# Second-half low parts on VectorE from PSUM, GpSimd on adjacency tiles alone, with counts, routing and fills moved (graph layer and expert layer, one core)

## The chip, the cores and the metric

One core of one Trainium2 chip runs the kernel. The metric is the device time of one launch in microseconds; the profiled execution has a span (first to last instruction) and a time with what lies around the span.

## The reference, cut to what matters

2048 rows of 256 values pass through a graph layer and then through an expert layer: each row goes to one of 8 experts (top 1 of the logits), and to a shared feed-forward layer of width 1024 besides.

```python
def layer(x, adj, W, b, gate_w, w1, w2, w3, sw1, sw2):
    deg = maximum((adj != 0).sum(-1), 1)
    xn = layernorm(x)
    pooled = rsqrt(deg) * ((adj + I) @ xn) * rsqrt(deg) + xn
    x = x + relu(pooled @ W + b)
    xf = layernorm(x)                                   # 2048 x 256
    w, idx = top_1(xf @ gate_w.T)                       # of 8 experts, weight softmax(w)
    y = sum_e [idx == e] * ((silu(xf @ w1[e].T) * (xf @ w3[e].T)) @ w2[e].T)
    y = y + gelu(xf @ sw1.T) @ sw2.T                    # the shared layer, width 1024
    return x + y
```

## The kernel before

**High and low parts.** Matmuls take fp32r operands, so an operand is split: ScalarE copies it to an fp32r tile (the high part), VectorE or GpSimd subtracts that from the original (the low part), and TensorE multiplies both. All that GpSimd splits has its original in SBUF.

**Tiles.** 2048 rows are NT = 16 tiles of 128, in NQ = 4 quarters. Quarter q of the graph layer sums over the 16 adjacency tiles (128x512 each): `adj_highs` on ScalarE (L667), `adj_lows` on GpSimd (L477), `agg_part` on TensorE (L1304 and L1306). Tiles 0 to 7 of quarters 2 and 3 are split ahead, in the shared stage before (LEAD = 8; AR = 4 of them in the first ring of slots). The raw tiles come two to a DMA ("chunk", NC = 8 a quarter) into RAW = 4 slots on SP's queue; a slot comes free when the low parts of its tiles are done and VectorE has counted it (`count_chunks`, L922 for the first chunk of a quarter and L925 for the others), so a late count delays a load.

**Order on TensorE.** Quarter 0, then for q = 1, 2, 3: quarter q of the sums (`agg_quarter`, with the transposes of the layer-normed rows of quarter q - 1 ahead of tile 12, L1262), gate, degrees, and for q = 1 and 2 a *shared stage* of 16 blocks of the shared layer (blocks 0 to 15, 16 to 31); after quarter 3 the last stage of 32 blocks (32 to 63, LAST = 32), with the routing of the last rows. Then 23 expert steps.

**A block m of the shared layer** is 128 columns of the width for 256 rows: `shared_up` (6 matmuls, L1405) into PSUM, gelu into `gel` (ScalarE, L726), its high part `gel_hi` (ScalarE, L730), its low part `gel_lo` (GpSimd, L490, from `gel` in SBUF), `shared_down` (4 matmuls, L1427 and L1429). TensorE issues up(m), down(m - 2), up(m + 1), and so on; `gel_hi` of block m waits until down(m - 2) is done, and the buffers hold two blocks. In a shared stage ScalarE and GpSimd do two blocks and then one adjacency tile of the next quarter, eight times.

**VectorE in a shared stage** finishes the graph layer, reads logits (`choose`), ranks (`read_ranks`) and positions (`place_rows`), adds the shared result of the first half to the rows (`add_shared`, L1042 and L1049), counts the first three chunks of the next quarter and adds the second half. In the quarter that follows it makes the variances of the rows (L860, L865), waits for the roots (`stds`, ScalarE L641), scales, adds the bias (L916) and counts on. ScalarE does `stds` after its tile 11 and then four `scaled_rows` (L647).

**GpSimd at the end of quarters 2 and 3** scatters four tiles of rows to `sorted_x` (L554) ahead of the next shared stage's first low part.

**The last stage.** GpSimd makes the low parts of blocks 32 to 55, with scatters between, and VectorE those from LAST + DVE_AT on. VectorE also splits chunks 0 to 7 of expert 0 (`low_chunk`, L1155), GpSimd the rest (`low`, L520). The routing tables end with `routed`. SP loads expert chunks (L417; each waits until an earlier chunk has been split, `elo_ok`), writes 8 fill blocks into `sorted_x` (L409) ahead of chunk MORE = 8, and loads the sorted rows of steps 0 to 2 (L425) behind chunks 11, 12 and 13, after waiting for `routed`, the scatters (L421) and the fills. TensorE transposes the rows of step 0 (L1262) ahead of block 63's up.

## Time and profile before

| | us |
|---|---|
| median of 3 runs (475.58 to 478.83) | 475.96 |
| time of the profiled execution | 476.37 |
| its span | 474.6 |
| TensorE matmul busy | 445.6 (94%) |
| GpSimd busy | 322.6 (68%) |
| VectorE busy | 255.2 (54%) |
| ScalarE busy | 208.4 (44%) |
| first shared stage | 81.3 to 109.3 |
| second shared stage | 134.4 to 163.2 |
| last shared stage | 188.4 to 241.0 |

The times of the stages are from the span's start. TensorE is the busiest engine nearly everywhere, so what counts is where it stands idle and who ends its wait. Matmuls overlap, so a stage's length is read from the starts of its matmuls and not from their busy time.

### The profile page before, as it was taken

The numbers are of one execution on the slowest core, as the hardware profiler recorded it, in microseconds if no ns is written. First come the engines' busy times: TensorE is split into PE (matmuls) and PEld (weight loads), VectorE is DVE, ScalarE is ACT, GpSimd is POOL, SyncE is SP. The second block draws the span as 40 slices with busy tenths as digits, with TensorE's granted clock in tenths as the row PEclk, the third lists the DMA queues.
The fourth block names the chain that finished last, engine by engine and source line by source line (L and its number), as shares of the span: only waits on it lengthen the run. The fifth ranks groups of instructions, "written<-read, shape, count | busy, mean of one in ns | idle before, by whom it ended". The sixth has DMA issues, their size and how long they took to land.

```text
span 474.6 us, 8852 instructions
## 1 busy us (share of the span) xinstructions
PE 445.6 (94%) x2635; PEld 381.7 (80%) x2636; DVE 255.2 (54%) x540; ACT 208.4 (44%) x462; POOL 322.6 (68%) x296
## 2 busy tenths in 40 slices
PE   7889999989999899999898999999999999999992
PEld 6779777878888788888787888888888888888872
DVE  5884979663767455888934433343334334433430
ACT  4777596655456354645442323232323222322330
POOL 3548975897488765779875498885677579883112
PEclk9999999999999899999999999999999999999997
DMA  8555534130440407685665999997898552663000
GB/s 272 205 176 182 159 107 136 55 110 24 134 135 1 134 2 254 228 310 207 195 200 151 377 353 378 339 341 240 305 330 303 184 203 36 75 79 44 2 0 0
DMA packets 39612, 82.61 MB, mean 174 GB/s; under 512 B 5024, under 2 KB 14752, under 8 KB 37536
## 3 DMA queue, kind: packets, MB, share of 16 engines
q1 hardware_dynamic: 27024, 47.60, 30.8%
q0 software_dynamic: 7536, 29.39, 20.2%
q10 hardware_dynamic: 5024, 5.27, 3.6%
q8 instruction: 15, 0.25, 0.2%
q14 instruction: 13, 0.11, 0.1%
HBM read 74.74 MB, written 8.41 MB: 175 GB/s over the span
## 4 chain that ended last, share of the span: by engine, by line
PE 72%; POOL 11%; DVE 6%; ACT 4%; issue 3%; DMA 2%; SPq 1%; POOLq 0%; ACTq 0%; DVEq 0%
PE bank L1486 26%; PE bank L1513 9%; PE bank L1304 9%; PE bank L1514 5%; PE bank L1306 4%; PE bank L1499 4%; POOL gel_lo L490 4%; PE bank L1405 4%; PE bank L1427 3%; PE bank L1262 2%; POOL a_lo L477 2%; POOL ering L520 2%; PE bank L1429 1%; PE bank L1288 1%; POOL sorted_x L554 1%
## 5 line engine op out<-in xcount | busy, mean ns | idle before, releaser
L1486 PE MATMUL bank<-ering,xsT_hi 128*128 x368 | 121.7, 402 | 1.4 <-POOL ering L520 1.4
L477 POOL TENSOR_TENSOR a_lo<-araw,a_hi 128x512 fp32r<-128x512 f32 x48 | 69.9, 1467 | 28.4 <-ACT a_hi L667 27.8
L1220 DVE SCALAR_TENSOR_TENSOR hid<-bank,xs,sil 128x512 f32<-128x512 f32 x46 | 34.5, 751 | 93.9 <-ACT sil L803 93.9
L1486 PEld LDWEIGHTS bank<-ering,xsT_hi 128*128 128x128 f32 x368 | 69.4, 189 | 17.8 <-issue 1.9
L1486 PE MATMUL bank<-ering,xsT_lo 128*128 x184 | 73.0, 396 | 0.0
L1304 PE MATMUL bank<-zz,a_hi 128*128 128x512 f32 x192 | 69.9, 404 | 2.4 <-POOL a_lo L477 2.4
L803 ACT ACTIVATE sil<-bank 128x512 f32<-128x512 f32 x46 | 27.5, 598 | 101.4 <-PE bank L1486 101.4
L520 POOL TENSOR_TENSOR ering<-eraw,ering 128x512 fp32r<-128x512 f32 x40 | 51.4, 1303 | 29.2 <-DMA ering<-in_experts 20.3
L1513 PE MATMUL bank<-ering,hidT_hi 128*128 x184 | 67.5, 407 | 1.2 <-DVE hidT_lo L1228 1.2
L520 POOL TENSOR_TENSOR ering<-eraw_more,ering 128x512 fp32r<-128x512 f32 x48 | 60.6, 1292 | 8.3 <-PE bank L1262 5.1
L625 POOL DMA_INDIRECT out<-y_rows,row_token x23 | 35.8, 1554 | 36.8 <-DVE y_rows L1236 31.4
L1427 PE MATMUL bank<-sw_r,gel_hi 128*128 128x512 f32 x128 | 50.4, 415 | 8.7 <-POOL gel_lo L490 6.9
L1306 PE MATMUL bank<-zz,a_lo 128*128 128x256 f32 x192 | 53.8, 280 | 0.0
L490 POOL TENSOR_TENSOR gel_lo<-gel,gel_hi 128x256 fp32r<-128x256 f32 x56 | 43.2, 778 | 14.9 <-ACT gel_hi L730 14.3
L1514 PE MATMUL bank<-ering,hidT_lo 128*128 x184 | 51.7, 281 | 0.0
L1304 PEld LDWEIGHTS bank<-zz,a_hi 128*128 128x128 f32 x192 | 36.1, 188 | 11.6 <-POOL a_lo L477 2.8
L1513 PEld LDWEIGHTS bank<-ering,hidT_hi 128*128 128x128 f32 x184 | 34.6, 188 | 8.7 <-issue 1.4
L925 DVE SCALAR_TENSOR_TENSOR count<-araw,count 128x1024 bf16<-128x1024 f32 x28 | 40.0, 1428 | 1.6
L1486 PEld LDWEIGHTS bank<-ering,xsT_lo 128*128 128x128 f32 x184 | 34.8, 189 | 7.3
L1405 PE MATMUL bank<-xfT_hi,sw_hi 128*128 128x256 f32 x128 | 37.3, 292 | 0.0
L1427 PEld LDWEIGHTS bank<-sw_r,gel_hi 128*128 128x128 f32 x128 | 24.7, 193 | 15.1 <-POOL gel_lo L490 6.7
L730 ACT ACTIVATE gel_hi<-gel 128x256 fp32r<-128x256 f32 x64 | 26.8, 418 | 22.5 <-PE bank L1429 22.2
(165 smaller groups left out, 931.1 us busy)
## 6 DMA issues: line engine op xcount, KB each, us to landing
araw<-in_adj_t SPq DMA_DIRECT2D x32, 512.0 KB, 4.5
eraw<-in_experts SPq DMA_DIRECT2D x48, 256.0 KB, 4.7
ering<-in_experts POOLq DMA_DIRECT2D x8, 1536.0 KB, 9.3
eraw_more<-in_experts SPq DMA_DIRECT2D x48, 256.0 KB, 5.9
ering<-in_experts POOLq DMA_DIRECT2D x8, 1024.0 KB, 7.1
ering<-in_experts POOLq DMA_DIRECT2D x8, 512.0 KB, 5.2
xs<-sorted_x ACTq DMA_DIRECT2D x20, 129.0 KB, 3.7
sw_raw<-in_sw_t ACTq DMA_DIRECT2D x2, 1024.0 KB, 7.5
```

Source lines behind the costliest of these rows:

```text
L477: pool.tensor_tensor(lo_part(s), araw[:, u // CJ, u % CJ, :], hi_part(s).bitcast(F32), ALU.subtract).then_inc(adj_lo_ok, 1)
L490: pool.tensor_tensor(gel_lo[:, u, :], gel[:, u, :], gel_hi[:, u, :].bitcast(F32), ALU.subtract).then_inc(sh_lo, 1)
L520: pool.tensor_tensor(ering[:, slot, 1, c * ECW:(c + 1) * ECW], raw, ering[:, slot, 0, c * ECW:(c + 1) * ECW].bitcast(F32), ALU.subtract).t ...
L625: pool.indirect_dma_start(out=out, out_offset=bass.IndirectOffsetOnAxis(ap=row_token[:, s:s + 1], axis=0), in_=y_rows[:, s, :], in_offset= ...
L925: dve.scalar_tensor_tensor(into, araw[:, r, :, :], 0.0, into, ALU.not_equal, ALU.add).then_inc(adj_counted, CJ)
L1304: pe.matmul(acc(q, it)[:, :], hi_part(s)[:, it * P:(it + 1) * P], zt, start=first, stop=False)
L1306: ins = pe.matmul(acc(q, it)[:, 0:D], lo_part(s)[:, it * P:(it + 1) * P], zt[:, 0:D], start=False, stop=False)
L1405: ins = pe.matmul(up_bank(m)[:, 0:HALF], w[:, k, ib * P:(ib + 1) * P], a[:, q % 2, k, half * HALF:(half + 1) * HALF], start=n == 0, stop=n ...
L1427: pe.matmul(shared_bank(hq, k)[:, :], gel_hi[:, m % 2, k * P:(k + 1) * P], sw2_r[:, ib, :, :].rearrange("p h d -> p (h d)"), start=ib == 0 ...
L1486: ins = pe.matmul(bank[2 * w + h][:, :], a[:, k, :], ering[:, bass.ds(slot, 1), part, at:at + BANK].rearrange("p a n -> p (a n)"), start=n ...
L1513: pe.matmul(bank[6][:, :], hidT_hi[:, k, :], w2, start=k == 0, stop=False)
L1514: ins = pe.matmul(bank[6][:, 0:D], hidT_lo[:, k, :], ering[:, bass.ds(slot, 1), 0, W2AT + k * D:W2AT + (k + 1) * D].rearrange("p a n -> p ...
```

## The change

- Blocks 8 to 15 of each of the first two shared stages: gelu goes to PSUM (`gel_in`, two banks that are free then), ScalarE makes `gel_hi` from there, and VectorE the low part (`shared_lows_from_psum`). GpSimd makes the low parts of blocks 0 to 7 alone, and after them `exp_of_z` and adjacency tiles 3 to 7.
- VectorE's order in these stages: the first half's sums are spread between the low parts, and the three counts come after the last low part.
- In quarters 2 and 3 ScalarE does `stds` ahead of tile 8 and the scaled rows after tiles 9 and 10; VectorE adds the bias after the count of chunk 3 and not before it.
- Last stage: GpSimd also makes the low parts of blocks 56 and 57 (DVE_AT 24 to 26). VectorE adds the shared result of the sixth half-quarter and splits chunks 4 to 7 before the later part of the routing tables.
- SP: three fills stay ahead of chunk 8, five go ahead of chunk 20; the sorted rows of steps 0 to 2 are loaded behind chunks 13, 14 and 15. ScalarE waits for all fills before its loop over the steps.

```diff
--- before.py
+++ after.py
@@ -183,9 +183,10 @@
     LAST = (NQ - 2) * 2 * NI
 
     EARLY_RANKS_AT, THIRD_RANKS_AT, XF_AT, GATE_AT, RANKS_AT = 9, 9, 8, 11, 14
-    DVE_AT = 24
+    DVE_AT = 26
     EARLY, MORE = 4, 8
-    FIRST_AT, FIRST_ROWS = EC - 1, 3
+    FIRST_AT, FIRST_ROWS = EC + 1, 3
+    FILLS_AT = 2 * EC - ER
     STORE_FROM = 3 * EC + ER
 
     with ExitStack() as ctx:
@@ -220,6 +221,10 @@
 
             stage = min(m // (2 * NI), NQ - 2)
             return bank[(4 if m >= (2 * NQ - 1) * NI else other(stage + 1)) + m % 2]
+
+        def gel_in(m):
+
+            return acc(m // (2 * NI) + 1, 1 - m % 2)[:, 0:HALF]
 
         def shared_bank(hq, k):
 
@@ -402,9 +407,9 @@
                 for c in range(EC):
                     n = e * EC + c
 
-                    if n == MORE:
+                    if n == MORE or n == FILLS_AT:
                         sp.wait_ge(counted, 1)
-                        for a in range(E):
+                        for a in range(FIRST_ROWS) if n == MORE else range(FIRST_ROWS, E):
                             row = sp.value_load(fill_row[0:1, a:a + 1], min_val=0, max_val=SPARE - P)
                             sp.dma_start(sorted_x[bass.ds(row, P), :], pad_row[:]).then_inc(filled, 16)
                     slot, to = raw_at(e, c)
@@ -418,7 +423,7 @@
                     if n == FIRST_AT:
                         sp.wait_ge(routed, 1)
                         sp.wait_ge(scattered, 16 * NT)
-                        sp.wait_ge(filled, 16 * (E + 1))
+                        sp.wait_ge(filled, 16 * (1 + FIRST_ROWS))
                     if FIRST_AT <= n < FIRST_AT + FIRST_ROWS:
                         i = n - FIRST_AT
                         row = sp.value_load(step_row[0:1, i:i + 1], min_val=0, max_val=SPARE)
@@ -562,12 +567,15 @@
                 if q >= 2:
                     scatter(q - 2, 0, QT)
                 if q < NQ - 1:
-                    for j in range(LEAD):
+                    pool.wait_ge(sh_lo, (q - 1) * 2 * NI)
+                    for j in range(AR):
                         shared_lows((q - 1) * 2 * NI + 2 * j, 2)
-                        adj_lows(q + 1, j, j + 1)
-                        if j == AR - 1:
-                            exp_of_z(q - 1)
-
+                        if j < AR - 1:
+                            adj_lows(q + 1, j, j + 1)
+                    exp_of_z(q - 1)
+                    adj_lows(q + 1, AR - 1, LEAD)
+
+            pool.wait_ge(sh_lo, LAST)
             shared_lows(LAST, 2)
             pool.wait_ge(agg_sum, NQ)
             pool.wait_ge(adj_counted, NQ * NT)
@@ -606,6 +614,7 @@
             scatter(3, 2, 3)
             shared_lows(LAST + 22, 2)
             scatter(3, 3, 4)
+            shared_lows(LAST + 24, 2)
 
             pool.wait_ge(elo_ok, MORE)
             for c in range(MORE, EC):
@@ -718,6 +727,21 @@
                                    xf_bank(q, b)[:, :].rearrange("p (t k n) -> p t k n", t=2, k=KD),
                                    ACT.Copy).then_inc(xfT_hi_ok, 1)
 
+            def shared_blocks_in_psum(first, n):
+
+                for m in range(first, first + n):
+                    q = m // (2 * NI) + 1
+                    if m % NI == 0:
+                        act.wait_ge(agg_free, (q + 1) * QT)
+                    if m % NI == 1:
+                        act.wait_ge(rank_read, q)
+                    act.wait_ge(sh_ps, m + 1)
+                    act.wait_ge(sh_lo, m - 1)
+                    act.activation(gel_in(m), up_bank(m)[:, 0:HALF], ACT.Gelu).then_inc(sh_gelu, 1)
+                    act.wait_ge(sh_gelu, m + 1)
+                    act.wait_ge(sh_used, m - 1)
+                    act.activation(gel_hi[:, m % 2, :], gel_in(m), ACT.Copy).then_inc(sh_hi, 1)
+
             def shared_blocks(first, n):
                 def one(u, m, early):
                     act.wait_ge(sh_ps, m + 1)
@@ -760,15 +784,17 @@
             for q in range(1, NQ):
                 if q == 1:
                     split_gate()
+                if q > 1:
+                    stds(NQ + q - 1)
                 for j in range(ring(q), NT - 1 if q == 1 else NT):
                     adj_highs(q, j, j + 1)
                     if q == 1 and AR + 2 <= j < AR + 10:
                         shared_piece_high(j - AR - 2)
-                    if j == ring(q) + 3:
+                    if q == 1 and j == AR + 3:
                         stds(NQ + q - 1)
-                    if ring(q) + 4 <= j < ring(q) + 6:
+                    if AR + 4 <= j < AR + 6 and q == 1 or LEAD + 1 <= j < LEAD + 3 and q > 1:
                         for i in range(2):
-                            scaled_rows((q - 1) * QT + 2 * (j - ring(q) - 4) + i, NQ + q - 1)
+                            scaled_rows((q - 1) * QT + 2 * (j - (AR + 4 if q == 1 else LEAD + 1)) + i, NQ + q - 1)
                 xfT_highs(q - 1)
                 if q == 1:
                     adj_highs(q, NT - 1, NT)
@@ -779,7 +805,10 @@
                     act.dma_start(sorted_x[SPARE:SPARE + P, :], pad_row[:]).then_inc(filled, 16)
                 if q < NQ - 1:
                     for j in range(LEAD):
-                        shared_blocks((q - 1) * 2 * NI + 2 * j, 2)
+                        if j < AR:
+                            shared_blocks((q - 1) * 2 * NI + 2 * j, 2)
+                        else:
+                            shared_blocks_in_psum((q - 1) * 2 * NI + 2 * j, 2)
                         adj_highs(q + 1, j, j + 1)
             shared_blocks(LAST, XF_AT)
             xfT_highs(NQ - 1)
@@ -832,6 +861,7 @@
             silus(0)
             rows_high(2)
             hid_highs(0)
+            act.wait_ge(filled, 16 * (1 + E))
             with act.Fori(0, (STEPS - 3) // XR) as i:
                 for u in range(XR):
                     step(i * XR + (1 + u), (1 + u) % XR)
@@ -1035,6 +1065,12 @@
                 settle()
                 dve.tensor_tensor(at, part(0), at, ALU.add).then_inc(logit_ok, 1)
 
+            def shared_lows_from_psum(first, n):
+                for m in range(first, first + n):
+                    dve.wait_ge(sh_hi, m + 1)
+                    dve.tensor_tensor(gel_lo[:, m % 2, :], gel_in(m), gel_hi[:, m % 2, :].bitcast(F32),
+                                      ALU.subtract).then_inc(sh_lo, 1)
+
             def first_sums(hq):
 
                 dve.wait_ge(sh_used, (hq + 1) * NI)
@@ -1108,11 +1144,11 @@
                 scales(NQ + q - 1)
                 if q == 1:
                     shared_pieces(1, 3)
-                else:
-                    add_bias(q)
                 count_chunks(q, 3, RAW)
                 if q == 1:
                     shared_pieces(3, 5)
+                else:
+                    add_bias(q)
                 count_chunks(q, RAW, RAW + 1)
                 if q == 1:
                     shared_pieces(5, 7)
@@ -1138,9 +1174,17 @@
                 logits(q - 1)
                 if q < NQ - 1:
                     choose(q - 1)
+                    second_half = (2 * q - 1) * NI
+                    dve.wait_ge(sh_lo, second_half)
+                    shared_lows_from_psum(second_half, 1)
                     read_ranks(q - 1)
+                    shared_lows_from_psum(second_half + 1, 1)
                     place_rows(q - 1)
-                    add_shared(2 * (q - 1))
+                    shared_lows_from_psum(second_half + 2, 1)
+                    first_sums(2 * (q - 1))
+                    shared_lows_from_psum(second_half + 3, 1)
+                    second_sums(2 * (q - 1))
+                    shared_lows_from_psum(second_half + 4, NI - 4)
                     count_chunks(q + 1, 0, 3)
                     add_shared(2 * (q - 1) + 1)
             choose(NQ - 2)
@@ -1178,6 +1222,9 @@
             step(dve.tensor_tensor(r_e[:, :, 0:E], per_e(tiles[:], E), upto[:], ALU.mult))
             step(dve.tensor_reduce(ends[:], r_e[:, :, 0:E], AX_X, ALU.add))
 
+            add_shared(2 * NQ - 3)
+            for c in range(EARLY, MORE):
+                low_chunk(c)
             step(dve.tensor_tensor(r_s[:], per_e(ends[:], STEPS), s_iota[:], ALU.is_le))
             step(dve.tensor_reduce(step_f[:], r_s[:], AX_X, ALU.add))
             step(dve.tensor_scalar(step_i[:], step_f[:], float(E - 1), None, ALU.min))
@@ -1198,9 +1245,6 @@
                                   xsT_hi[:].bitcast(F32), ALU.subtract).then_inc(xsT_lo_ok, 1)
                 dve.tensor_copy(row_token[:, bass.ds(n - 1, 1)], xs[:, u, D:D + 1]).then_inc(token_ok, 1)
 
-            for c in range(EARLY, MORE):
-                low_chunk(c)
-            add_shared(2 * NQ - 3)
             dve.wait_ge(sh_lo, LAST + DVE_AT)
             for m in range(LAST + DVE_AT, NB):
                 if m == NB - 2:
@@ -1208,9 +1252,9 @@
                 dve.wait_ge(sh_hi, m + 1)
                 dve.tensor_tensor(gel_lo[:, m % 2, :], gel[:, m % 2, :], gel_hi[:, m % 2, :].bitcast(F32),
                                   ALU.subtract).then_inc(sh_lo, 1)
+                if m == LAST + DVE_AT:
+                    first_sums(2 * NQ - 2)
                 if m == LAST + DVE_AT + 1:
-                    first_sums(2 * NQ - 2)
-                if m == LAST + DVE_AT + 2:
                     second_sums(2 * NQ - 2)
 
 
```

## Rows read from the trace of the kernel before

**Rows 1.** Busy time of each engine by stretch: two shared stages, quarter 2 between them.
```profile
81.30:109.27 27.97, 24.94 (x186) 22.10 (x182) 16.98 (x38) 16.71 (x41) 24.00 (x25) 1.00 0.31 97
109.27:134.43 25.16, 25.16 (x154) 21.49 (x153) 14.60 (x26) 11.72 (x22) 14.70 (x12) 1.00 0.29 85
134.43:163.24 28.81, 26.11 (x185) 23.18 (x182) 16.96 (x38) 16.76 (x41) 25.23 (x27) 0.94 0.28 91
```

**Rows 2.** Timeline of TensorE, first stage: start, duration, instruction, [idle before <- releaser].
```profile
95.04 0.39 PE L1427 MATMUL bank<-sw_r,gel_hi 128*128 128x512 f32 x1
...
95.73 0.28 PE L1405 MATMUL bank<-xfT_hi,sw_hi 128*128 128x256 f32 x1
...
104.69 0.50 PE L1427 MATMUL bank<-sw_r,gel_hi 128*128 128x512 f32 x1 [1.77 <-POOL gel_lo L490]
...
110.66 0.40 PE L1304 MATMUL bank<-zz,a_hi 128*128 128x512 f32 x1
```

**Rows 3.** Timeline of GpSimd, second half of the first stage.
```profile
100.69 2.28 POOL L477 TENSOR_TENSOR a_lo_more<-araw,a_hi_more 128x512 fp32r<-128x512 f32 x1
102.94 2.39 POOL L490 TENSOR_TENSOR gel_lo<-gel,gel_hi 128x256 fp32r<-128x256 f32 x2
```

**Rows 4.** Timeline of VectorE, second half of the first stage.
```profile
99.00 1.11 DVE L922 TENSOR_SCALAR count<-araw 128x1024 bf16<-128x1024 f32 x1
100.25 3.81 DVE L925 SCALAR_TENSOR_TENSOR count<-araw,count 128x1024 bf16<-128x1024 f32 x2
```

**Rows 5.** Groups by form: x count | busy us, mean ns | idle before.
```profile
L1197 DVE TENSOR_TENSOR xsT_lo<-bank,xsT_hi 128x256 fp32r<-128x256 f32 x23 | 9.6, 415 | 1.9 <-ACT xsT_hi L797 1.9
...
L1209 DVE TENSOR_TENSOR gel_lo<-gel,gel_hi 128x256 fp32r<-128x256 f32 x8 | 6.2, 784 | 1.7 <-ACT gel_hi L730 1.7
...
L730 ACT ACTIVATE gel_hi<-gel 128x256 fp32r<-128x256 f32 x64 | 26.8, 418 | 22.5 <-PE bank L1429 22.2
...
L667 ACT ACTIVATE a_hi<-araw 128x512 fp32r<-128x512 f32 x48 | 29.9, 628 | 14.5 <-PE bank L1306 14.5
```

**Rows 6.** Timeline of VectorE, start of quarter 2.
```profile
109.47 0.76 DVE L1042 TENSOR_TENSOR resid<-bank,resid 128x256 f32<-128x256 f32 x2 [5.42 <-PE bank L1429]
...
112.36 0.38 DVE L865 BATCH_NORM_AGGREGATE mv<-stats 128x2 f32<-128x6 f32 x4
```

**Rows 7.** Timeline of ScalarE, quarter 2.
```profile
115.73 1.28 ACT L641 ACT_TABLE_LOAD   x1
117.03 0.30 ACT L641 ACTIVATE std<-mv,eps 128x4 f32<-128x4 f32 x1
```

**Rows 8.** Chain that ended last, in order of time: transposes ahead of tile 12.
```profile
126.08 0.87 PE bank L1262 x8
```

**Rows 9.** Timeline of GpSimd, quarter 2 and the start of the second stage.
```profile
119.46 1.55 POOL L477 TENSOR_TENSOR a_lo_more<-araw,a_hi_more 128x512 fp32r<-128x512 f32 x1 [0.23 <-ACT a_hi_more L667]
127.32 2.54 POOL L477 TENSOR_TENSOR a_lo_more<-araw,a_hi_more 128x512 fp32r<-128x512 f32 x2 [6.31 <-ACT a_hi_more L667]
...
136.34 1.45 POOL L490 TENSOR_TENSOR gel_lo<-gel,gel_hi 128x256 fp32r<-128x256 f32 x2 [0.51 <-ACT gel_hi L730]
```

**Rows 10.** Timeline of TensorE, last stage: block 56's down, step 0's rows.
```profile
232.87 0.47 PE L1427 MATMUL bank<-sw_r,gel_hi 128*128 128x512 f32 x1 [1.57 <-DVE gel_lo L1209]
...
239.30 0.38 PE L1262 MATMUL bank<-ident,xs 128*128 128x128 f32 x2
```

**Rows 11.** Timeline of VectorE, last stage: chunks 4 to 7.
```profile
225.87 4.14 DVE L1155 TENSOR_TENSOR ering<-eraw,ering 128x512 fp32r<-128x512 f32 x4
```

**Rows 12.** Timeline of GpSimd, last stage: chunks 8 to 11.
```profile
231.19 5.56 POOL L520 TENSOR_TENSOR ering<-eraw,ering 128x512 fp32r<-128x512 f32 x4 [0.92 <-DMA eraw<-in_experts]
```

**Rows 13.** Timeline of SP's queue, last stage: eight fills, sorted rows of step 0.
```profile
218.29 8.85 SPq L409 DMA_DIRECT2D sorted_x<-pad_row  x8
...
234.12 0.34 SPq L425 DMA_DIRECT2D xs<-sorted_x  x1
```

**Rows 14.** DMA issues between 228 and 240: x count, KB, median us to landing.
```profile
xs<-sorted_x SPq DMA_DIRECT2D x3, 129.0 KB, 3.8
```

## Prediction

> **What bounds the kernel now.** I read first the busy shares by stretch: a shared stage takes 27.97 us the first time and 28.81 the second, and TensorE is idle for part of both; in the quarter between them, 25.16, it is not [rows 1]. Then TensorE's own timeline: from block 7's down at 95.04 to block 10's up at 95.73 a down takes 0.69, an up the same, so a block is worth 1.40; but block 12's down waits 1.77 for a low part of GpSimd [rows 2]. GpSimd's and VectorE's timelines beside it say why: GpSimd's adjacency tile takes 2.28, where two take 2.54 in the quarter [rows 9], and its next two low parts 2.39, while VectorE's two counts stretch to 3.81, where the first count, which has one input in SBUF, takes 1.11 [rows 3, 4]. The reader is to see in these rows a stage that GpSimd bounds, and two engines that hold each other up just where GpSimd has no time to spare. The second stage's granted clock is 0.94 [rows 1]: for a while TensorE ran at 1.2 and not 2.4 GHz, after the same wait.
>
> **Stage one.** From 95.04 on TensorE has downs 7 to 15 and ups 10 to 15 to do: 15 pieces of 0.70 are 10.5. The last down must wait for its own high and low part behind block 13's down, with one down of cover: high part 0.42, low part 0.415 [rows 5], some 0.3 of signals (my estimate from the gaps between such instructions) make 1.15; less 0.70, 0.45 is exposed. 95.04 + 10.5 + 0.45 + 0.1 = 106.1, where the quarter now starts at 109.27 [rows 1]: **-3.15**. The low part's price decides: VectorE takes 415 ns for 128x256 with one operand in PSUM, 784 ns from two SBUF tiles [rows 5]. I take the first, whose form this is; the upper bound too fits into 1.40 and would cost 0.4 once a stage. What VectorE does between the low parts (positions some 2 us, sums 0.76 a pair [rows 6]) fits: I find block 10's low part, behind `place_rows`, within 0.1 of its due time, all others early. ScalarE has two passes of 0.42 a block and a tile of 0.63 every second block [rows 5], 2.3 in 2.8.
>
> On the low part's form the Trainium skill speaks against the change: "VectorE: DVE Perf Modes", the section on the TRN2 errata, gives VectorE 62 cycles more per operation from PSUM than from SBUF, an estimate of 0.065 us a block. By that rule the stage would lose 0.065 more at its last block; by the rows nothing.
>
> **Stage two.** The same, and the low clock goes with the wait that I take for its cause: 28.81 - (27.97 - 3.15) = **-4.0**. If the wait isn't its cause it stays: 0.85 less gain [rows 1].
>
> **Quarters 2 and 3, where the counts go.** T is a quarter's start. VectorE ends its last low part at T - 0.9, the first count (1.11) at T + 0.25; one GpSimd tile (the seventh, from T - 0.8) is in the way until T + 0.5, then come two counts of 1.25 each (3.81 less a tile of 1.27, halved [rows 4, 9]), to T + 3.0. Sums and variances took 3.27 from 109.47 to 112.74 [rows 6], so they end at T + 6.3, 2.8 later than now. ScalarE's roots now stand ahead of tile 8, behind them ScalarE's high parts, behind those GpSimd's low parts and TensorE. The table load of 1.28 stands ahead of the root and needs nothing from VectorE (115.73, then the root at 117.03 [rows 7]), so it is long done: tile 8's high part starts at T + 6.6, its low part could at T + 7.2. Beside GpSimd's tiles VectorE then counts chunk 3, adds the bias and counts twice. A count costs GpSimd 1.0 (2.28 less 1.27 [rows 3, 9]), an add at most 0.28 (1.55 less 1.27 [rows 9]). Tile 14's low part ends at 7.2 + 1.0 + 7 x 1.25 + 4 x 0.28 + 2 x 1.0 = T + 20.1. TensorE wants it at 14 x 1.39 + 0.87 = T + 20.3 (110.66 less 109.27 for a tile [rows 1, 2]; transposes [rows 8]). It holds by 0.2. Tile 15 ends at T + 21.3; now it ends at 129.86, T + 20.6, and the scatters behind it were done 0.51 before the second stage's first low part [rows 9], so they come 0.2 to 0.3 late: +0.3 a quarter. Bounds: nothing, if the adds slip between; if each count blocks for its whole 1.25 and each add for 0.3, tile 14 ends at T + 20.8, 0.5 late, and the scatters take 0.35 more: +0.85 a quarter. So 0.6 to 1.7 for both, and I take **+1.1**, the middle, as 2.39 less 1.45 for two low parts (0.94 [rows 3, 9]) points to the lower end and 3.81 to the upper.
>
> The Trainium skill's "SBUF — State Buffer", Who interferes with whom, has the two engines exclude each other when VectorE reads two SBUF inputs and GpSimd reads SBUF, the second fully blocked. By it the quarters would cost 1.7. The trace's 3.81 for two counts agrees, its 1.0 per count on GpSimd is a little less.
>
> What costs nothing: chunk 7 is loaded when chunk 3 has been counted, at T + 8.2 and now near T + 13.3, so GpSimd's tiles 14 and 15 no longer wait for it (6.31 idle now [rows 9]). Were that later again, it would be on TensorE at once.
>
> **The last stage.** GpSimd's last scatter ends at 231.19 - 0.92 = 230.3 [rows 12], block 56's low part follows at once, and TensorE's wait of 1.57 [rows 10] goes: its down comes at 231.15 and not 232.87, and step 0's transposes could come at 237.6 and not 239.30. But they need the sorted rows of step 0, and these move behind two more chunks on SP; chunk 12 waits for chunk 8's split, chunk 13 for chunk 9's. GpSimd now first does blocks 56 and 57 (to 231.9, all in old times), then four chunks at 1.39 [rows 12]: chunk 9's split ends at 234.8, SP issues chunk 13, reads the row number and issues the load at 236.0, now 234.12 [rows 13]. With 3.8 to landing [rows 14] that is 239.8: TensorE waits 2.2, and step 0 begins 0.5 later than now, though all before it was 1.7 early. Bounds by a landing 1 us faster or slower: -0.5 to +1.5. Splitting chunks 4 to 7 (4.14 beside GpSimd [rows 11]) moves to where GpSimd has blocks and scatters without a gap: I add 0.3 (bounds 0 and 1). For TensorE's 2.2 us of idleness I add 0.4, half the price of the low clock above, since it came after one of two long waits. Together **+1.2**. Hidden: the routing tables end 5.7 later, near 225.9 + 5.7 = 231.6 [rows 11], still ahead of the load; the five fills (8.85 for eight [rows 13], 1.1 each) stand ahead of chunk 20, the down weights of expert 1, due behind step 2's up. Without that cover the fills would cost 5.5. The steps themselves are untouched.
>
> **Sum.** -3.15 - 4.0 + 1.1 + 1.2 = -4.85 against the profiled execution's 476.37, which lies 0.4 above the median. I take the difference over: 475.96 - 4.85 = 471.1.
>
> **Rivals.**
> 1. *The quarters give the gain back* (0.22). For it: 0.2 of slack at tile 14. If the first count too excludes GpSimd's seventh tile, everything moves by 1.2 more on top of the upper bound: 2.0 a quarter, 4.0 and not 1.1, 474.0. Against it: the first count stayed at 1.11 beside GpSimd's work [rows 4].
> 2. *The sorted rows land in time* (0.18): then the last stage gives -0.4 and no low clock, 1.6 less than my +1.2: 469.5. For it: the landing alone decides, and 1 us of it does half.
> 3. *VectorE's low parts are late* (0.08): `place_rows` reads two SBUF inputs twice and may wait 1.27 for a tile [rows 9]; block 10 is 1.3 late in each stage: 473.7.
> 4. *Slower* (0.07): ScalarE's root becomes the wait. From variances at T + 6.6 on each microsecond later goes onto TensorE, in both quarters. At T + 9.0 they have eaten the 4.85; at T + 11.5 it is 480.9. Against it: VectorE's 3.27 [rows 6] meets nothing of GpSimd's.
> 5. *The change doesn't do what it says* (0.03): ScalarE's passes through PSUM are so slow that ScalarE bounds the stages as GpSimd did: 476.5. Against it: it has 0.5 to spare in 2.8.
>
> **How the numbers follow.** My own case has 0.42 and runs from 469.8 to 472.6. The range runs from below rival 2, 468.0, over rivals 1 and 3 to 474.8; rivals 4 and 5 and the ends of the others are left out, under 0.2. Within 1% (4.76 us, about what a measurement of this kernel can tell from no change) begins at 471.2. Below it lie 0.26 of my own case's 0.42 and all of rival 2: 0.44. Slower by over 1% is the far part of rival 4 and what I don't see: 0.04. The rest, 0.52, is within 1%.
>
> **What the profile would show.** Right: first stage near 24.8, second the same at clock 1.00; VectorE's low parts at 0.42; quarters of 25.2 to 26; TensorE waiting about 2 us for a DMA at step 0's transposes; ScalarE idle some 6 us ahead of its root. Wrong: quarters above 26.5 with TensorE waiting for tiles 9 to 14 (rival 1), no wait at step 0 (rival 2), block 10's down a microsecond late (rival 3), a second stage still at clock 0.94.

## The result and the profile after

| | before | after |
|---|---|---|
| median, us | 477.22 (11 runs, 475.51 to 481.15) | 472.80 (11 runs, 471.62 to 475.31) |
| ratio to before | | 0.9902, 95% interval 0.988 to 0.9924 |
| profiled execution: time, span | 476.37, 474.6 | 472.11, 470.4 |

The changed kernel is faster by 0.98%, 4.4 us by the medians and 4.26 by the profiled executions; forecast were 4.85. That lies just inside the 1% to which the forecast gave 0.52. The forecast time was 471.1 and the measured one is 472.80: 0.4 of the difference is the smaller gain and 1.3 the kernel before, whose median is 477.22 over 11 runs and was 475.96 over the three that the forecast started from.

The busy times by stretch, cut at the starts of TensorE's stages (columns as in [rows 1]: stretch, length, then busy time and count of TensorE's matmuls, its weight loads, VectorE, ScalarE, GpSimd, granted clock, DMA share, GB/s):

```profile
81.58:106.50 24.92, 24.18 (x184) 21.95 (x181) 15.64 (x45) 16.93 (x42) 16.34 (x17) 1.00 0.15 48
106.50:132.26 25.76, 25.53 (x154) 21.48 (x153) 22.32 (x28) 10.59 (x22) 18.47 (x11) 1.00 0.47 152
132.26:157.50 25.24, 24.15 (x184) 21.93 (x181) 15.65 (x45) 17.09 (x42) 18.25 (x19) 1.00 0.09 34
157.50:183.23 25.73, 25.49 (x155) 21.61 (x153) 22.34 (x28) 10.57 (x22) 18.39 (x12) 1.00 0.52 170
183.23:234.45 51.22, 47.89 (x356) 42.69 (x352) 44.37 (x106) 25.29 (x63) 44.23 (x51) 1.00 0.65 220
```

The stages that took 27.95 and 28.81 take 24.92 and 25.24, and the clock of the second is 1.00. The quarters between them, 25.16 and 25.15 before, have grown to 25.76 and 25.73. What TensorE still waits for at the places that the change touched and ahead of step 1, from its timeline (start, duration, instruction, idle before and who ended it):

```profile
105.69 0.50 PE L1471 MATMUL bank<-sw_r,gel_hi 128*128 128x512 f32 x1 [0.29 <-DVE gel_lo L1071]
128.65 0.51 PE L1348 MATMUL bank<-zz,a_hi_more 128*128 128x512 f32 x1 [0.23 <-POOL a_lo_more L482]
135.46 0.47 PE L1471 MATMUL bank<-sw_r,gel_hi 128*128 128x512 f32 x1 [0.80 <-POOL gel_lo L495]
...
186.30 0.47 PE L1471 MATMUL bank<-sw_r,gel_hi 128*128 128x512 f32 x1 [0.58 <-POOL gel_lo L495]
...
234.45 0.44 PE L1306 MATMUL bank<-ident,xs 128*128 128x128 f32 x2 [1.66 <-DMA xs<-sorted_x]
...
247.00 0.50 PE L1530 MATMUL bank<-ering,xsT_hi 128*128 x1 [1.37 <-issue]
```

The wait of 1.77 in the stage is gone; 0.29 is left at its last down. Three new ones stand in its place: tile 15 of each quarter (128.65, and the same at 179.66), the first low part of the next stage (0.80 and 0.58; it was 0.39 and 0.37), and the sorted rows of step 0 (1.66). The last line, the pause ahead of the loop over the steps, is not new: it was 1.38 before. The first two new ones have one source, which GpSimd's and VectorE's timelines of quarter 2 show side by side:

```profile
113.94 6.44 POOL L482 TENSOR_TENSOR a_lo<-araw,a_hi 128x512 fp32r<-128x512 f32 x4 [6.56 <-ACT a_hi L676]
120.34 8.25 POOL L482 TENSOR_TENSOR a_lo_more<-araw,a_hi_more 128x512 fp32r<-128x512 f32 x4
128.79 1.97 POOL L559 DMA_INDIRECT sorted_x<-rows,pos  x1 [0.19 <-issue]
...
133.60 0.96 POOL L559 DMA_INDIRECT sorted_x<-rows,pos  x1 [0.30 <-issue]
```

```profile
106.37 3.46 DVE L955 SCALAR_TENSOR_TENSOR count<-araw,count 128x1024 bf16<-128x1024 f32 x2
...
112.63 0.38 DVE L895 BATCH_NORM_AGGREGATE mv<-stats 128x2 f32<-128x6 f32 x4
...
113.69 1.23 DVE L955 SCALAR_TENSOR_TENSOR count<-araw,count 128x1024 bf16<-128x1024 f32 x1
114.83 5.83 DVE L946 TENSOR_TENSOR rows<-rows,bias 128x256 f32<-128x256 f32 x4
120.59 4.53 DVE L955 SCALAR_TENSOR_TENSOR count<-araw,count 128x1024 bf16<-128x1024 f32 x2
...
126.24 3.43 DVE L955 SCALAR_TENSOR_TENSOR count<-araw,count 128x1024 bf16<-128x1024 f32 x2
```

GpSimd begins tile 8 only at T + 7.44 (T = 106.50), 6.56 idle, and from there VectorE is in its way nearly all the time: four tiles take 6.44 and the next four 8.25, where a tile alone is 1.27 [rows 9]. Four bias adds take 5.83, 1.46 each, where one took 0.42 alone (at 117.65 in the kernel before): each ends about 0.3 after the tile beside it, so it was held until that tile was done. The last tile ends at T + 22.1, and the fourth scatter leaves at 134.56, when the stage has long begun.

### The profile page after: what moved, and what is told of

It reads as the page before. It is cut to its first block, busy times and chain, and to the rows that moved or that the text cites. A ratio compares the mean times of both kernels' runs of the same rounds, so it can differ in the third digit from the quotient of the medians.

```text
span 470.4 us, 8858 instructions
## 1 busy us (share of the span) xinstructions
PE 444.2 (94%) x2635; PEld 380.3 (81%) x2636; DVE 269.1 (57%) x554; ACT 206.8 (44%) x462; POOL 318.2 (68%) x282
## 3 DMA queue, kind: packets, MB, share of 16 engines
q0 software_dynamic: 7536, 29.39, 20.3%
## 4 chain that ended last, share of the span: by engine, by line
PE 66%; POOL 13%; DVE 10%; ACT 4%; issue 3%; DMA 2%; POOLq 0%; SPq 0%; DVEq 0%; ACTq 0%
PE bank L1530 28%; PE bank L1557 9%; PE bank L1449 5%; PE bank L1558 5%; PE bank L1543 4%; POOL a_lo L482 4%; PE bank L1471 4%; POOL a_lo_more L482 3%; PE bank L1348 3%; POOL sorted_x L559 2%; POOL gel_lo L495 2%; PE bank L1473 2%; PE bank L1306 2%; DVE stats L890 2%; DVE count L955 2%
## 5 line engine op out<-in xcount | busy, mean ns | idle before, releaser
L482 POOL TENSOR_TENSOR a_lo<-araw,a_hi 128x512 fp32r<-128x512 f32 x48 | 72.4, 1524 | 37.2 <-ACT a_hi L676 37.1
L1471 PE MATMUL bank<-sw_r,gel_hi 128*128 128x512 f32 x128 | 48.6, 402 | 3.5 <-POOL gel_lo L495 2.8
L955 DVE SCALAR_TENSOR_TENSOR count<-araw,count 128x1024 bf16<-128x1024 f32 x28 | 44.4, 1585 | 1.3
L495 POOL TENSOR_TENSOR gel_lo<-gel,gel_hi 128x256 fp32r<-128x256 f32 x42 | 31.2, 750 | 12.4 <-ACT gel_hi L754 11.6
L1350 PEld LDWEIGHTS bank<-zz,a_lo 128*128 128x128 f32 x192 | 36.3, 189 | 0.0
L1473 PE MATMUL bank<-sw_r,gel_lo 128*128 128x256 f32 x128 | 35.9, 281 | 0.0
```

The source lines that it names most:

```text
L482: pool.tensor_tensor(lo_part(s), araw[:, u // CJ, u % CJ, :], hi_part(s).bitcast(F32), ALU.subtract).then_inc(adj_lo_ok, 1)
L495: pool.tensor_tensor(gel_lo[:, u, :], gel[:, u, :], gel_hi[:, u, :].bitcast(F32), ALU.subtract).then_inc(sh_lo, 1)
L955: dve.scalar_tensor_tensor(into, araw[:, r, :, :], 0.0, into, ALU.not_equal, ALU.add).then_inc(adj_counted, CJ)
L1350: ins = pe.matmul(acc(q, it)[:, 0:D], lo_part(s)[:, it * P:(it + 1) * P], zt[:, 0:D], start=False, stop=False)
L1471: pe.matmul(shared_bank(hq, k)[:, :], gel_hi[:, m % 2, k * P:(k + 1) * P], sw2_r[:, ib, :, :].rearrange("p h d -> p (h d)"), start=ib == 0 ...
L1473: ins = pe.matmul(shared_bank(hq, k)[:, 0:D], gel_lo[:, m % 2, k * P:(k + 1) * P], sw2_r[:, ib, 0, :], start=False, stop=ib == NI - 1)
```

## The experiments

All kernels measured, by stretch. "Last" is from the last stage's start to step 0's up, "0 to 2" and "2 to 6" from the up of one step to that of the other, all in the profiled execution; then its time and the median of all runs of that kernel.

| kernel | stage 1 | quarter 2 | stage 2 | quarter 3 | last | 0 to 2 | 2 to 6 | profiled | median |
|---|---|---|---|---|---|---|---|---|---|
| before | 27.95 | 25.16 | 28.81 | 25.15 | 52.64 | 20.19 | 38.23 | 476.37 | 477.22 |
| after | 24.92 | 25.76 | 25.24 | 25.73 | 53.13 | 20.17 | 38.42 | 472.11 | 472.80 |
| e1 | 24.87 | 25.76 | 25.27 | 25.76 | 51.70 | 20.24 | 39.36 | 471.36 | 472.10 |
| e2 | 24.90 | 25.47 | 25.01 | 25.57 | 54.77 | 21.71 | 38.13 | 473.66 | 472.07 |
| e3 | 24.87 | 25.59 | 24.88 | 25.48 | 52.94 | 21.71 | 38.13 | 472.49 | 472.40 |
| e4 | 26.04 | 26.08 | 26.43 | 26.06 | 54.13 | 22.19 | 38.38 | 477.57 | 477.02 |
| e5 | 24.92 | 25.75 | 25.34 | 25.76 | 53.33 | 21.67 | 38.10 | 473.43 | 473.34 |
| e6 | 24.91 | 25.77 | 25.24 | 25.74 | 52.86 | 21.65 | 38.14 | 472.31 | 471.73 |
| e7 | 24.91 | 25.74 | 25.26 | 25.77 | 51.63 | 21.82 | 38.17 | 472.72 | 472.24 |
| e8 | 24.91 | 25.47 | 24.87 | 25.47 | 51.63 | 21.77 | 39.19 | 473.62 | 471.11 |
| e9 (after again) | 24.91 | 25.76 | 25.24 | 25.71 | 53.46 | 21.70 | 38.11 | 474.89 | 474.89 |
| e10 | 24.91 | 25.27 | 25.19 | 25.16 | 51.54 | 20.34 | 39.24 | 470.59 | 470.97 |
| e11 | 24.91 | 25.27 | 24.91 | 25.27 | 51.61 | 20.24 | 38.34 | 469.27 | 469.63 |

The last two columns alone would mislead. The table shows which stretch an edit touched; "0 to 2" is 20.2 or 21.7 for a reason of its own (e9), and in e2 and e4 the same reason lengthens "last".

**e1: sorted rows one chunk earlier.**

```diff
-    FIRST_AT, FIRST_ROWS = EC + 1, 3
+    FIRST_AT, FIRST_ROWS = EC, 3
```

> The changed kernel with one edit: the sorted rows of steps 0 to 2 are loaded one chunk of the expert weights earlier on SP's queue. Theory: the 1.66 us that TensorE waits for a DMA at step 0's transposes come from the place of this load alone; the routing tables end at 228.35 and the load can go out near 229.2 and not 231.03, lands near 232.7, and the transposes begin near 232.8 and not 234.45. All of the 1.6 stays to the end: profiled time about 470.5 for 472.1. Rival: what is late next (the expert weights split by GpSimd, or the steps' own rows) takes it back: the transposes come earlier, step 0's up or step 1's does not, gain under 0.5.

The load left at 229.29 and not 231.03, the wait of 1.66 was gone, and "last" fell by 1.43. But the time fell by 0.75 only: steps 2 to 6 took 0.94 more. TensorE's timeline, the steps that lost (windows, columns as above), and GpSimd's timeline ahead of step 6:

```profile
264.51:274.43 9.92, 9.79 (x53) 8.03 (x52) 3.95 (x8) 3.28 (x8) 8.10 (x7) 1.00 1.05 384
283.99:294.33 10.34, 9.76 (x52) 8.05 (x51) 4.37 (x9) 3.68 (x8) 8.88 (x9) 1.00 1.00 352
```

```profile
294.33 0.50 PE L1530 MATMUL bank<-ering,xsT_hi 128*128 x1 [0.58 <-POOL ering L525]
```

```profile
285.90 1.29 POOL L525 TENSOR_TENSOR ering<-eraw,ering 128x512 fp32r<-128x512 f32 x1 [1.44 <-DMA ering<-in_experts]
...
288.97 6.26 POOL L525 TENSOR_TENSOR ering<-eraw_more,ering 128x512 fp32r<-128x512 f32 x5
```

Step 6 waits for the eighth chunk of an expert to be split, GpSimd waits for that expert's weights to land, and the DMA engines have a share of 1.0 meanwhile. The theory held up to step 0. Something late did take gain back, as the rival had it, but not where it looked: steps 0 and 1 began earlier, and the loss is ahead of steps 4 and 6, with a gain of 0.75 left and not under 0.5.

**e2: the root behind tile 11.**

```diff
-                if q > 1:
-                    stds(NQ + q - 1)
...
-                    if q == 1 and j == AR + 3:
+                    if j == ring(q) + 3:
                         stds(NQ + q - 1)
-                    if AR + 4 <= j < AR + 6 and q == 1 or LEAD + 1 <= j < LEAD + 3 and q > 1:
+                    if ring(q) + 4 <= j < ring(q) + 6:
...
```

> The changed kernel, but ScalarE's root in quarters 2 and 3 stands behind its high part of tile 11 again, and the scaled rows behind tiles 12 and 13. VectorE's order is that of the changed kernel. Theory: what makes the quarters 0.6 long is GpSimd's late start, since tile 8's high part waits behind a root that waits for the variances (T + 6.5), while its data are there near T + 4; with the root behind, GpSimd starts tile 8 near T + 4.2 and not T + 7.4, has 3 us of slack against the counts, the quarters go back to 25.2 and the scatters end before the next stage's first low part: 1.2 to 1.8 less than the changed kernel, about 470.6. Rival: the root is needed where it is, because count 3 and the load of chunk 7 hang on it: quarters 25.8 or longer, no gain or a loss.

GpSimd's timeline and TensorE's only wait from quarter 2 to the second stage's first downs:

```profile
110.56 2.55 POOL L482 TENSOR_TENSOR a_lo<-araw,a_hi 128x512 fp32r<-128x512 f32 x2 [3.60 <-ACT a_hi L676]
114.05 2.54 POOL L482 TENSOR_TENSOR a_lo<-araw,a_hi 128x512 fp32r<-128x512 f32 x2 [0.94 <-ACT a_hi L676]
116.70 3.63 POOL L482 TENSOR_TENSOR a_lo_more<-araw,a_hi_more 128x512 fp32r<-128x512 f32 x2
122.34 3.52 POOL L482 TENSOR_TENSOR a_lo_more<-araw,a_hi_more 128x512 fp32r<-128x512 f32 x2 [2.01 <-ACT a_hi_more L676]
```

```profile
134.51 0.47 PE L1469 MATMUL bank<-sw_r,gel_hi 128*128 128x512 f32 x1 [0.44 <-POOL gel_lo L495]
```

Tile 8 starts at T + 4.5 (T = 106.07), the first four tiles cost 1.27 each, no tile is late and the scatters leave in time. Yet the quarter took 25.47, not 25.16: TensorE's first twelve tiles took 16.97 where the changed kernel's took 16.65, without a wait in either. That is a rate, not a stall (see the end); less that 0.32, the quarter is 25.15. The whole from stage 1 to the last stage was 0.70 shorter; twice 0.3 of rate on top, the order is worth 1.3, the lower part of what was expected. e11 had the same order without that rate: 25.27, 24.91, 25.27, 1.29 less than the changed kernel.

The profiled time is nevertheless 1.55 longer than the changed kernel's, and not 470.6 as expected. Step 1's low clock (e9) adds 1.54 to it, and "last" took 1.64 more: the wait for the sorted rows was 2.00 there, and behind it TensorE's clock fell, which it did not behind the 1.66 of the changed kernel:

```profile
233.84 0.69 PE L1304 MATMUL bank<-ident,xs 128*128 128x128 f32 x2 [2.00 <-DMA xs<-sorted_x]
```

```profile
234.00:237.00 3.00, 3.00 (x13) 2.81 (x14) 0.91 (x3) 1.46 (x4) 2.83 (x3) 0.50 0.88 280
```

From these transposes to step 0's up it is 3.05, and 1.91 in the changed kernel. Of the six kernels with this wait (1.54 to 2.00), e2 and e4 (1.93) show the low clock behind it, e9 (1.94), e5 (1.85), the changed kernel and e3 do not.

**e3: counts with one input.** Chunks 3 to 7 of quarters 2 and 3 are counted without adding to what was counted, so degrees and rows differ from the reference's.

```diff
-                if first:
+                if first or (q >= 2 and n >= q * NC + 3):
+                    dve.wait_ge(adj_counted, n * CJ)
                     dve.tensor_scalar(into, araw[:, r, :, :], 0.0, None, ALU.not_equal)
```

> The changed kernel, but in quarters 2 and 3 the counts of chunks 3 to 7 are done in the form of the first count, which has one input in SBUF and does not add to what was counted: the degrees, and with them the rows, are not the reference's. Everything else, waits too, stays. Theory (VectorE's two inputs in SBUF and GpSimd exclude each other): a GpSimd tile beside such a count takes 1.3 again, the four tiles of 6.44 and the four of 8.25 become about 6 and 5.3, a count takes 0.7 to 1.1; quarters 25.2, scatters on time, 1.2 to 1.8 less than the changed kernel. Rival (any access of VectorE to SBUF holds GpSimd up, or the late root alone makes the stall): tiles as before, quarters still 25.7.

GpSimd's timeline, then VectorE's:

```profile
114.22 5.92 POOL L482 TENSOR_TENSOR a_lo<-araw,a_hi 128x512 fp32r<-128x512 f32 x4 [6.55 <-ACT a_hi L676]
120.10 6.10 POOL L482 TENSOR_TENSOR a_lo_more<-araw,a_hi_more 128x512 fp32r<-128x512 f32 x4
```

```profile
120.34 3.47 DVE L953 TENSOR_SCALAR count<-araw 128x1024 bf16<-128x1024 f32 x2
...
126.21 1.51 DVE L953 TENSOR_SCALAR count<-araw 128x1024 bf16<-128x1024 f32 x2
```

The stretch of two counts in the first line has a gap of 0.14 in it: they took 1.78 and 1.56. With the late root kept, cheaper counts alone brought GpSimd's last tile forward from T + 22.1 to T + 19.4; no tile and no scatter was late (25.59 less 0.32 of the same rate is 25.27). So lateness is start plus contention, and either half undone is enough. But the theory's reason was wrong by half: one-input counts do wait for tiles, 1.78 and 1.56 beside them and 0.68 alone, and the tiles they met took 1.73 where one alone is 1.27. They cost GpSimd less because they are shorter (0.7 and not 1.2), not because they leave it alone. The Trainium skill says as much in "SBUF — State Buffer", Who interferes with whom: a one-input `tensor_scalar` in a mode that uses both ports takes the shared pair too, and whoever comes second is blocked for the whole instruction; the rows agree.

**e4: GpSimd keeps all low parts, counts still behind them.** GpSimd's and ScalarE's orders in the stages are those of the kernel before; the lines shown are VectorE's.

```diff
-                    dve.wait_ge(sh_lo, second_half)
-                    shared_lows_from_psum(second_half, 1)
...
-                    shared_lows_from_psum(second_half + 4, NI - 4)
+                    dve.wait_ge(sh_lo, second_half + NI)
                     count_chunks(q + 1, 0, 3)
```

> The changed kernel, but all low parts of the first two shared stages stay with GpSimd, from SBUF, two blocks and a tile in turn, as in the kernel before; VectorE's three counts still come after the last low part, and quarters and last stage are those of the changed kernel. Theory: the stages gained from two things, and the counts' move is the larger: without them beside it GpSimd needs 1.45 for two low parts and 1.27 for a tile, 2.72 in 2.8 us of TensorE, so a stage takes 25.3 to 26 (27.95 and 28.81 before, 24.92 and 25.24 in the changed kernel). Rival: GpSimd cannot keep up even alone (its 2.72 leave nothing for the signals between it and ScalarE), and the low parts' move is what was needed: stages of 27 or more.

Stages of 26.04 and 26.43, at clock 1.00: of the 3.03 and 3.57 that the stages gained, 1.9 and 2.4 come from taking three counts out of GpSimd's way (0.86 of the 2.4 is the low clock of the kernel before), 1.1 and 1.2 from VectorE's low parts. That is the worth of the second move with the first one made; the low parts moved alone, with the counts left in the stage, were not run. Neither pure theory: GpSimd alone nearly keeps up, and where exp_of_z (1.05) or the end of the stage meets it, TensorE waits 0.4 to 0.5. Its quarters, 26.08 and 26.06, are the longest of all; the first count there begins at T - 0.76, beside a tile, and takes 1.71, so that all behind it comes later. Over the whole kernel little is left: its median, 477.02 over 10 runs, is 0.7 below that of the kernel before in the same session (ratio 0.9971, interval 0.9943 to 0.9998). With the quarters and the last stage as changed, the counts' move alone earns little more than they cost.

**e5: VectorE's low parts from SBUF.**

```diff
-                    dve.tensor_tensor(gel_lo[:, m % 2, :], gel_in(m), gel_hi[:, m % 2, :].bitcast(F32),
+                    dve.tensor_tensor(gel_lo[:, m % 2, :], gel[:, m % 2, :], gel_hi[:, m % 2, :].bitcast(F32),
...
```

> The changed kernel, but in blocks 8 to 15 of the first two stages gelu goes to SBUF as before, and VectorE makes the low parts from two SBUF tiles. Theory: it is the form with one operand in PSUM that keeps a low part at 0.42; from SBUF every second one meets a GpSimd tile and takes 0.8 to 1.3 (784 ns on average in the last stage [rows 5]), which reaches the path of TensorE's downs: stages of 25.2 to 26 in place of 24.9 and 25.2, GpSimd's tiles above 1.3. Rival: the cover of one down (0.7) hides that, and PSUM isn't needed: stages within 0.1 of the changed kernel's.

VectorE's timeline, two blocks of the first stage:

```profile
100.97 0.73 DVE L1068 TENSOR_TENSOR gel_lo<-gel,gel_hi 128x256 fp32r<-128x256 f32 x1 [0.17 <-ACT gel_hi L754]
102.37 0.42 DVE L1068 TENSOR_TENSOR gel_lo<-gel,gel_hi 128x256 fp32r<-128x256 f32 x1 [0.67 <-ACT gel_hi L754]
```

The mechanism is there, 0.73 beside a tile and 0.42 without, and it costs nothing that shows: 24.92 and 25.34, and GpSimd's tiles stay at 1.29 to 1.30. The last low part of a stage, the only one without cover, met no tile. The rival is right, and PSUM is not what made the gain.

**e6: the last stage as before.**

```diff
-    DVE_AT = 26
+    DVE_AT = 24
-    FIRST_AT, FIRST_ROWS = EC + 1, 3
+    FIRST_AT, FIRST_ROWS = EC - 1, 3
...
-            shared_lows(LAST + 24, 2)
```

> The changed kernel with the last stage of the kernel before (GpSimd's low parts to block 55, all eight fills ahead of chunk 8, sorted rows behind chunks 11 to 13, VectorE's order). Theory: the 1.57 of wait at block 56 is back, the wait for the sorted rows at step 0 is gone; last stage 50.9 to step 0's transposes and 1.7 on to its up, so step 0 begins 0.5 earlier than in the changed kernel: the last stage's own edits cost 0.5. Rival: they are worth something because the steps after them start from a better place (weights' chunks, clock): the end comes at the changed kernel's time or later.

"Last" took 52.86, against 53.13, 53.46 and 53.33 in three executions of the changed last stage (after, e9, e5): its edits cost 0.3 to 0.6, since the wait at block 56 that they take away, 1.04 here, comes back larger as the wait for the sorted rows. The steps don't pay for it, as the rival had it: from step 2 on they are as long as elsewhere (38.14 for "2 to 6", the changed kernel 38.42 and 38.11).

**e7, e8, e11: stores later, and the edits joined.**

```diff
-    STORE_FROM = 3 * EC + ER
+    STORE_FROM = 5 * EC
-                    if STORE_FROM <= n < STORE_FROM + 3 * NT and (n - STORE_FROM) % 6 == 0:
+                    if STORE_FROM <= n < STORE_FROM + 2 * NT and (n - STORE_FROM) % 4 == 0:
...
```

e7 is e1 with this; e8 is e7 with e2's edit; e11 is e1 with e2's edit, without the stores'.

> The first experiment (sorted rows one chunk earlier) with one edit more: the eight output stores of SP's queue, between chunks 40 and 82, go between chunks 60 and 88. In the first experiment step 0 began 1.64 earlier than in the changed kernel, but 0.9 was lost again in steps 4 and 6 while the DMA engines were at a share of 1.0. Theory: the stream of expert weights is the bound there; three stores of 129 KB at about 370 GB/s leave the full stretch, 0.35 each, so step 6 begins up to 1.0 earlier, steps 4 and 6 take 9.54, time about 469.3 for 470.1 or so. Rival: what is late is GpSimd's splitting or the free ring slot, not the rate: steps 4 and 6 stay at 9.9 and 10.3.

> The changed kernel with sorted rows one chunk earlier, stores later, and ScalarE's root behind tile 11: all that the experiments so far point to. Theory: the gains add until the stream of weights is the bound: last stage begins 1.2 earlier than in the changed kernel, step 0 near 233.7, steps as before, 468.5 to 469.5. Rival: a wall of the weights' stream near step 6 (294.3 in the first experiment, 294.95 in the changed kernel) lets nothing through: 470.5 to 471.5.

> The changed kernel with the sorted rows one chunk earlier and the root behind tile 11, the stores where they were. Against the kernel with stores later too, this tells what the stores are worth. Theory: with the stores in the full stretch the eighth chunk of expert 2 is split 1 us later, so that step 6 waits 0.8 to 1.8 where there is no low clock in step 1. Rival: the stores make no difference: that chunk is split as long after the loads of expert 2's first parts as in the kernel with stores later (40.5 us).

Later stores were worth nothing that shows. From the issue of the expert's first weights to the end of its eighth split it is 40.2 us in e1 and 39.9 in e11 (stores where they were), 38.3, 40.5 and 40.4 in e7, e8 and e10 (stores later); steps 2 to 6 lost 1 us in e8 and e10 and nothing in e11. e7 lost nothing either (38.17), but had the low clock in step 1, which puts all later steps off by 1.5, so it can't tell. A wall at a fixed time, e8's rival, is out: step 6 began at 292.09 in e11, ahead of 294.3. I take it that the stream's own spread of up to 2 us decides whether step 6 waits; no run isolates that. e8's profiled execution is the longest of its seven (473.62, against a median of 471.11); it had the low clock twice, in the first 20 us and in step 1. e11's gains add: quarters, stage 2 and scatters 1.29, "last" 1.52, together 2.81 of the 2.84 between the profiled times. Its median of 469.63 (4 runs, 469.15 to 470.38) is the lowest of all; ratio to before 0.9824, interval 0.9788 to 0.9861, which doesn't meet the changed kernel's 0.988 to 0.9924. Medians of different sessions differ by themselves (472.80 and 474.89 for the changed kernel), so for the other kernels but e4, at 471.0 to 473.3, the order follows from the stretches and not from the medians.

**e9: the changed kernel again, e10: e8 with filler on TensorE.**

> The changed kernel once more, unaltered, for a second profiled execution. Two things have come and gone in the profiles so far without an edit that would explain them: step 2's start comes 9.54 behind step 1's in three kernels and 10.9 to 11.1 in seven, with the granted clock at 0.50 just before; and four of TensorE's aggregation matmuls take 0.693 in some quarters and 0.707 in others, which is 0.3 a quarter. Theory: both are drawn anew in each execution, so here at least one of them differs from the changed kernel's first profile, though the code is the same; stages and waits are the same within 0.1. Rival: they belong to the kernel: all as in its first profile (9.54, 0.693, 0.693).

Windows of the first profile of the changed kernel, then of its second:

```profile
0.00:20.00 20.00, 15.67 (x98) 14.06 (x100) 13.70 (x45) 10.95 (x28) 8.50 (x24) 1.00 0.72 256
...
249.00:251.00 2.00, 2.00 (x10) 1.63 (x9) 0.27 (x1) 0.60 (x1) 2.00 (x3) 1.00 0.43 116
```

```profile
0.00:20.00 20.00, 16.17 (x90) 14.62 (x92) 12.22 (x44) 9.39 (x24) 7.94 (x24) 0.91 0.73 256
250.00:252.00 2.00, 2.00 (x6) 1.51 (x6) 0.32 (x1) 0.00 (x0) 2.00 (x2) 0.50 0.52 190
```

Same code, 2.8 us apart: TensorE ran at 1.2 GHz for a while in the first 20 us and again in step 1, about 1.5 us each time. Every stage and quarter agrees within 0.02, "last" within 0.33. For the clock the theory holds; the matmul rate was the same in both. The runs without a profile fit: of the changed kernel's 18 runs the seven with a mean clock of 0.993 to 0.995 took 471.6 to 472.1, the five at 0.987 took 474.9 to 475.8. The kernel before took 476.2 to 478.2 at 0.993 and 0.994 in the experiments' sessions, so its distance is not made by the clock.

```diff
+                    if isinstance(s, int) and s == 0:
+                        keep_clock_up(4 if h == 0 else 10)
```

> The last kernel of the second call (rows earlier, stores later, root behind tile 11) with 4 and 10 transposes more on TensorE in step 0, between and behind the transposes of the hidden rows, where it stands idle for 0.59 and 1.37 to 1.6 ahead of the loop over the steps; they write to a bank that has been read. Theory: the low clock in step 1 follows from these pauses; with filler in them the clock stays at 1.00, step 2 comes 9.54 behind step 1, 1.4 less than there, while the filler costs under 0.3, as it lies in the pauses. Rival: the pause ahead of the loop is the sequencer's own and comes behind the filler: step 1 is 1 us later and the clock drops as before.

The filler lay in the pauses (1.63 in e8 became 0.49) and cost at most 0.1 ("0 to 2" 20.34, and 20.24 in e11), and the clock stayed up; it did so in e11 without filler too. Whether filler helps is open: it would take many executions to tell.

## Why the sum of the prediction held and its parts did not all

Its -4.85 against a measured -4.26, step by step, with the measured stretches:

- **Stage one, -3.15:** measured -3.03. Low parts took 0.42, the last down waited 0.29, block 10's low part was not late (rival 3 is out). The credit was misplaced though: e4 shows that two thirds of it is the counts' move, and e5 that the operand in PSUM, on which the price rested, isn't needed. The 784 ns from two SBUF tiles [rows 5] were not the price of that form but held waits for GpSimd: without a tile beside it, it takes 0.42 too.
- **Stage two, -4.0:** -3.57; with the 0.41 by which the scatters came later, counted under the quarters, -3.98. The clock was 1.00, as it was in e4 with GpSimd's low parts kept, and no kernel without the counts in the stage shows a second stage more than 0.43 longer than the first. In the kernel before the clock was down behind the wait of 1.76 at 157.82:

```profile
160.00:162.00 2.00, 2.00 (x8) 1.45 (x6) 0.00 (x0) 0.94 (x3) 0.93 (x2) 0.50 0.22 83
```

That 0.86 was counted on as if it came each time. Its first stage had the same wait, 1.77, and kept its clock, and e2 and e9 show that the clock falls behind like waits in some executions and not in others. The kernel before was profiled once, so how often those 0.86 are there to be gained is open: up to that much of the agreement can be luck.

- **Quarters, +1.1 within 0.6 to 1.7:** +0.60 and +0.58, and 0.41 and 0.21 at the first low parts behind them, +1.8: just above the upper bound. The step that failed is the count of what lies beside GpSimd's tiles. I put three counts there, and there were four: with tiles and counts holding each other up, the count of chunk 6 (126.24) began together with tile 15 and held it up by a microsecond. And GpSimd began at T + 7.44 and not 7.2. Tile 15, not 14, was the late one: due at T + 21.7, expected at 21.3, ended at 22.1. One misreading did little harm: the first count's 1.11 [rows 4] was taken as its own length, and by rival 1 as a sign that it doesn't meet GpSimd. It takes 0.68 alone (105.55 in the changed kernel), so it had waited in the kernel before; and GpSimd's tile that it met took 1.61 and not 1.27. The second choice that failed was to give the root's new place no price, because TensorE had slack: it took GpSimd's head start of 3 us, and e2 and e11 show that this is most of what the quarters cost (1.29 of 1.8). By the Trainium skill's rule of full exclusion ("SBUF — State Buffer", Who interferes with whom) the sum was 1.7; measured are 1.8, so that was the better guide.
- **Last stage, +1.2:** +0.28 beyond the 0.21 of scatters. The term that was worked out held: step 0 0.5 later, the load at 231.03 (236.0 less the 5.16 by which the stage began earlier is 230.84), a wait of 1.66 for 2.2, as it landed in 3.4 and not 3.8. The 0.3 for the splits didn't show. The 0.4 for the clock didn't show in this profile, but the thing priced is real: in e2 and e4, two of the six kernels with the wait, the low clock came behind it and cost 1.1 to 1.2. That it stayed away here is luck.
- **The steps, 0:** +0.38, ahead of steps 5 and 17 above all, and the first stage began 0.26 later. "Untouched" was true of the code and not of the time: from 264 to 304 the DMA engines have a share of 0.96 to 1.07, and who reaches that stretch earlier waits in it. e1, e8 and e10 took 0.8 to 1.3 more there than the kernels that didn't wait.

So the quarters cost 0.7 more, the last stage 0.9 less, the steps and the start 0.6 more than forecast, near enough to each other to leave 0.6 in the sum. The total agrees better than its parts, and that is luck: errors of 0.6 to 0.9 with different signs. Rival 1 was right in kind, not in size (0.9 a quarter, not 2.0), rival 2 fell with the wait of 1.66, and rivals 4 and 5 never came near: the root stood at T + 6.54, close to the forecast.

## What to carry to other kernels

When work is moved off a loaded engine, ask what the engine that it excludes does at that hour: here moving three counts a stage was worth 4.3 in the stages (0.86 of it the low clock) and moving the low parts 2.3 on top, and the counts' new place, with the late root, took 1.8 back. An instruction put ahead in an in-order queue is free only if nothing behind it could have started; ScalarE's root hid 3 us of readiness. And look for the next stream at full rate behind the place you speed up, because gains can end there.

## What the runs showed of the hardware

- The low clock (1.2 GHz) comes and goes between executions of the same kernel, in the first 20 us and behind the pauses of 0.59 and 1.3 to 1.6 ahead of the loop: "0 to 2" was 20.2 or 20.3 in five profiles and 21.7 to 22.2 in eight. It came behind the wait for the sorted rows in two kernels of six. Most of a kernel's spread here, 471.6 to 476.1 over all runs of the changed one, goes with it: the lowest times have the highest mean clock (e9). The Trainium skill, "TensorE: Matmul & The Clock Gate", Part 1, also calls the number of slow matmuls at a kernel's start variable from run to run.
- At a granted clock of 1.00 four aggregation matmuls took 0.693 or 0.707, whole quarters at one or the other, 0.3 us a quarter: 0.707 in 12 of the 16 quarters of e1 to e8, in none of the ten of the other five profiles. What sets it is open.
- A one-input count took 0.68 at 105.55, where it met no running tile, 1.11 in the kernel before [rows 4], and 1.56 and 1.78 beside tiles in e3.
- ScalarE's table load ran at 105.71, 7.3 us ahead of the root (113.04) that was waiting for VectorE, so a late root pays for no table.
